# DMA transposes in place of TensorE transposes for attention outputs and expert products, in a two-layer macaron block

## The chip, the cores and the metric

The kernel is one program on one core of a Trainium2 chip. The metric is the time of an execution on the device in microseconds (us); several executions are timed, and the median is compared.

## The reference

The input is `x`, 4 sequences of 512 tokens, 128 wide, in 32 bits. Every stage adds to `x` (LN is a layer norm without weights):

```python
x = x + 0.5 * ffn(LN(x))       # W1, W2 made ternary; 128 -> 512 -> 128, relu
x = x + attn0(LN(x))           # RMS norm, 16 heads of 64, causal, gated by sigmoid(x @ Wg)
x = x + 0.5 * ffn(LN(x))       # the same weights again
x = x + 0.5 * moe(LN(x))       # 8 experts, the top 2 of each token
x = x + attn1(LN(x))           # layer norm with gamma and beta, 16 heads of 64, causal
x = x + 0.5 * moe(LN(x))       # the same experts
```

In attention, `out = softmax(q k^T) v` of all heads is laid side by side (1024 wide) and multiplied by `Wout` (1024 to 128). In `moe`, an expert computes `h = silu(xs @ W1[e]) * (xs @ W3[e])`, 512 wide, and `y = h @ W2[e]`, where `xs` is the token times its softmax weight; `y` is added to the token.

## The kernel before

**Numbers.** Matrix products are nearly as precise as 32 bits, in 16-bit operands: every operand is split into a high 16-bit part (a cast, mostly on ScalarE) and a low one (the value less the high part, on VectorE or GpSimd), and a product is three matmuls: high by high, high by low, low by high (`split_mm`, L1696 to L1703). The matmul contracts over the partitions, so the stationary operand must have the contracted axis on its partitions: a result that lies token by token has to be transposed before it can be multiplied by the next weight. TensorE does this with a matmul against the identity in 32 bits, from SBUF into PSUM; then ScalarE casts the transposed high part out of PSUM, and VectorE subtracts for the low one.

**Order of the work.** Each engine runs its own stream of instructions, written out by hand in the same shape, and semaphores tie them together. The stages are: first feed-forward; `attention(0)`; `moe(0)`; `attention(1)`; `moe(1)`. Norms, the second feed-forward, the routing and the loading of weights are put into turns of the attentions (tables `FILL`, `STATS`) and into iterations of the expert loops (`carried`). DMAs are issued by SyncE (SP) in one stream, the gathers and scatters of the expert tiles by GpSimd (POOL).

**Attention.** An item is one pair of heads of one sequence: 4 x 8 = 32 items. There are 36 turns t. In turn t item t is projected to q, k and v (`p`), item t-1 has its row maxima (`m`), item t-2 its scores and exponentials (`s`), item t-3 its outputs (`v`), item t-4 its output projection (`o`). TensorE's order in a turn is:

```python
scores(0); maxima(0); project_q(); project_k()  # k here, unless late_k
turn_outputs()                                  # L1926: 4 transposes of O32 into PSUM bank 7
scores(1); maxima(1)                            # scores(1) waits for the first exponential (L972)
project_k()                                     # here if late_k: a turn with no entry in FILL
project_v(); filled(); scores(2); maxima(2)
outputs(0); max_rows(); outputs(1); project_out()
```

`turn_outputs` (L1929) waits for VectorE to have divided the outputs of the turn before into `O32` (L1361). ScalarE casts the high part (`turned_high`, L1005), after its first exponential (L972) and the casts of q. VectorE makes the low part (`turned_low`, L1332) in its order after the second group of maxima (`maxima(1)`, L1308) and before the third. `project_out` (L1933) waits for that low part, `s_otl_sb`, and multiplies by `WOh` and `WOl` (L1698 to L1700). The PSUM banks 6 and 7 hold the outputs; bank 7 holds the transposed outputs in between, so `outputs(1)` waits for `s_otl_sb` of the item before (L1913). GpSimd makes most casts and low parts of the exponentials (L782, L784).

**Experts.** Tokens are sorted by expert into tiles of 128 rows, 46 tiles for each `moe`. GpSimd gathers the rows of a tile (L835) four tiles ahead and scatters the results eight iterations later (`OUT_LAG`, L843). In iteration t of `run_tiles` (L535) the stages run with lags 0, 1, 2 and 3: `turned_token` (TensorE transposes the tile, ScalarE and VectorE split it), `up` (two `split_mm` of 512 columns into banks 1 and 2; ScalarE's `gate`, L1124, applies silu, VectorE's `product`, L1662, multiplies into `G32`), `turned_product` (L2128: four 32-bit transposes into bank 3 or 4; ScalarE's `product_high`, L1130; VectorE's `product_low`, L1668) and `down` (twelve matmuls, L2140 to L2142; ScalarE's `result`, L1138). `up` of a tile waits for the gate and the product of the tile before, since all tiles use the same two banks.

**SyncE.** Its stream loads inputs and weights (L564 to L592), stores normalised tokens as rows in HBM for the gathers (L610), loads the expert results (L618) and stores the output (L603, L630), each behind a wait for its data.

## Time and profile before

| | us |
|---|---|
| three runs | 1001.63, 1004.79, 1005.98 |
| median | 1004.79 |
| span of the profiled execution (first to last instruction) | 1000.9 |
| attention(0), turns 0 to 35, roughly | 35 to 363 |
| moe(0) | 364 to 526 |
| attention(1) | 526 to 839 |
| moe(1) | 840 to 989 |
| busy: TensorE, VectorE, GpSimd, ScalarE | 897, 792, 735, 674 |

The profiled execution's own time is its span and what lies around it, which isn't shown apart; the span is 3.9 us below the median of the runs. An engine's busy time counts its instructions from start to end; TensorE's matmuls overlap, so a row of four may be "busy" for less than four times one. "PEld" is the load of the stationary operand. A row of the timeline has start, duration, engine, line, operation, what is written and read, and the count of merged instructions; in brackets stands how long the engine was idle before, and which instruction ended that.

### The profile page before, as it was taken

What the parts mean: (1) busy time and instruction counts of PE and PEld (TensorE: products, weight loads), DVE (VectorE), ACT (ScalarE), POOL (GpSimd) and SP (SyncE); (2) the same over time, 40 slices, a digit from 0 to 9 for tenths busy, and PEclk for the clock granted to TensorE, in tenths of its full rate; (3) what the DMA queues carried; (4) which work ended last, traced back from release to release, by engine and by line L of the source; (5) the groups of instructions that cost most, each with busy time, mean ns of one, the idle gap of its engine ahead of it and who ended that gap; (6) DMA issues with size and microseconds to landing.
All of it is one profiled execution on the core that took longest, in us unless ns stands there. A gap on an engine that the chain in (4) does not pass through costs nothing.

```text
span 1000.9 us, 33897 instructions
## 1 busy us (share of the span) xinstructions
PE 897.1 (90%) x13160; PEld 640.5 (64%) x13160; DVE 792.1 (79%) x2394; ACT 673.5 (67%) x1183; POOL 734.7 (73%) x685
## 2 busy tenths in 40 slices
PE   5789999999999879899987899999999985998884
PEld 3467676776777656566654676777677764666663
DVE  6889898888889877777656889888888887866563
ACT  6688888878877626556555787767767762545552
POOL 6789989889887745666545999878888883666662
PEclk9999999999999979999999999999999997999997
DMA  5201011010030001122111000000000001121222
GB/s 153 78 10 45 3 45 45 3 45 2 3 107 3 2 20 39 52 43 85 38 30 51 3 3 3 12 3 2 13 3 3 13 2 30 41 43 44 86 62 82
DMA packets 21118, 33.79 MB, mean 34 GB/s; under 512 B 4578, under 2 KB 10466, under 8 KB 20964
## 3 DMA queue, kind: packets, MB, share of 16 engines
q1 hardware_dynamic: 13728, 18.50, 5.9%
q0 software_dynamic: 5888, 12.07, 4.8%
q8 instruction: 110, 1.80, 0.8%
q10 hardware_dynamic: 1348, 1.05, 0.3%
q14 instruction: 44, 0.36, 0.1%
HBM read 22.44 MB, written 9.18 MB: 32 GB/s over the span
## 4 chain that ended last, share of the span: by engine, by line
PE 63%; DVE 18%; ACT 6%; issue 6%; POOL 3%; another core or an unknown queue 2%; DMA 1%; SPq 0%; POOLq 0%; DVEq 0%; ACTq 0%
PE ps L1698 8%; PE ps L1889 8%; PE ps L1700 8%; PE ps L1699 7%; DVE arena L1308 4%; PE ps L1919 3%; PE ps L2128 3%; PE ps L1853 3%; PE ps L1920 3%; PE ps L1921 3%; PE ps L2140 2%; PE ps L2141 2%; PE ps L2142 2%; PE ps L1864 2%
## 5 line engine op out<-in xcount | busy, mean ns | idle before, releaser
L784 POOL TENSOR_TENSOR arena<-arena 128x1024 f16<-128x1024 f32 x190 | 344.9, 1816 | 86.2 <-ACT arena L980 75.9
L1308 DVE CUSTOM_DVE_ANT_0 arena<-ps,mask_qk 128x512 bf16<-128x512 f32 (+3 forms) x512 | 224.4, 485 | 25.0 <-PE ps L1853 23.8
L972 ACT ACTIVATE arena<-ps,lift 128x1024 f32<-128x1024 f32 (+1 forms) x192 | 186.7, 972 | 85.0 <-PE ps L1899 82.2
L1889 PE MATMUL ps<-arena 64*128 64x512 f16 (+3 forms) x1536 | 148.5, 299 | 10.2 <-ACT arena L972 6.8
L835 POOL DMA_INDIRECT arena<-x_rows,arena x92 | 92.6, 1006 | 88.5 <-PE ps L2103 43.7
L1919 PE MATMUL ps<-arena 128*128 128x65 f16 x1280 | 130.9, 195 | 0.2 <-DVE arena L1332 0.2
L1920 PE MATMUL ps<-arena 128*128 128x64 f16 x1280 | 130.4, 193 | 0.0
L1921 PE MATMUL ps<-arena 128*128 128x65 f16 x1280 | 130.0, 194 | 0.0
L843 POOL DMA_INDIRECT y_rows<-arena x92 | 90.8, 987 | 49.0 <-ACT arena L1138 26.1
L1919 PEld LDWEIGHTS ps<-arena 128*128 128x128 f16 x1280 | 117.4, 98 | 8.4 <-issue 0.5
L1920 PEld LDWEIGHTS ps<-arena 128*128 128x128 f16 x1280 | 117.9, 99 | 0.2 <-issue 0.2
L1921 PEld LDWEIGHTS ps<-arena 128*128 128x128 f16 x1280 | 117.9, 98 | 0.0
L782 POOL CAST arena<-arena 128x1024 f16<-128x1024 f32 x124 | 103.6, 835 | 0.0
L1662 DVE SCALAR_TENSOR_TENSOR arena<-ps,arena 128x512 f32<-128x512 f32 x92 | 68.8, 748 | 29.1 <-ACT arena L1124 16.0
L1889 PEld LDWEIGHTS ps<-arena 64*128 64x128 f16 x1536 | 52.1, 94 | 53.1 <-ACT arena L972 22.3
L1668 DVE TENSOR_TENSOR arena<-ps,arena 128x512 f16<-128x512 f32 x92 | 63.1, 686 | 26.1 <-ACT arena L1130 18.4
L1130 ACT ACTIVATE arena<-ps 128x512 f16<-128x512 f32 x92 | 55.3, 601 | 42.1 <-PE ps L2128 24.7
L2140 PE MATMUL ps<-E2h,arena 128*128 x368 | 71.4, 222 | 11.1 <-DVE arena L1668 6.0
L1124 ACT ACTIVATE arena<-ps,arena 128x512 f32<-128x512 f32 x92 | 63.4, 689 | 18.5 <-PE ps L1700 15.1
L1853 PE MATMUL ps<-arena 64*128 64x512 f16 (+3 forms) x512 | 66.2, 296 | 7.7 <-DVE arena L1308 6.6
L2142 PE MATMUL ps<-E2h,arena 128*128 x368 | 71.1, 219 | 0.0
L2141 PE MATMUL ps<-E2l,arena 128*128 x368 | 71.0, 219 | 0.0
(288 smaller groups left out, 2695.9 us busy)
## 6 DMA issues: line engine op xcount, KB each, us to landing
stage<-in_L_ffn_W SPq DMA_DIRECT2D x4, 1024.0 KB, 5.3
arena<-y_rows SPq DMA_DIRECT2D x14, 256.0 KB, 3.6
x_rows<-XN SPq DMA_DIRECT2D x8, 256.0 KB, 2.1
arena<-x_rows,arena POOLq DMA_INDIRECT x92
y_rows<-arena POOLq DMA_INDIRECT x92
stage<-in_L_attn_Wkv SPq DMA_DIRECT2D x2, 512.0 KB, 8.3
X<-in_L_attn_tokens SPq DMA_DIRECT2D x3, 256.0 KB, 5.1
out_x<-X SPq DMA_DIRECT2D x3, 256.0 KB
```

What stands on the lines that cost most here:

```text
L782: g.tensor_copy(PH[:, b, :, cols], P32[:, :, cols]).then_inc(s_ph_pool, 1)
L784: g.tensor_tensor(PL[:, b, :, cols], P32[:, :, cols], PH[:, b, :, cols], ALU.subtract).then_inc(s_pl, 1)
L835: g.indirect_dma_start(XG[:, t % XRING, :], None, x_rows[t // HT], bass.IndirectOffsetOnAxis(ap=row_i[:, 0, t:t + 1], axis=0)).then_inc(s_ ...
L972: a_.activation(P32[:, :, UNIT_AT[u]:UNIT_AT[u] + UNIT_W[u]], ps[:, 4:6, 0:UNIT_W[u]], ACT.Exp, bias=lift[:]).then_inc(s_ex_p, 1)
L1308: v_.tensor_tensor_reduce(masked[:, x, 0:w], ps[:, 2 + x, at:at + w], mask_qk[:, CH - w:CH], 1.0, NEG, ALU.add, ALU.max, accum_out=MX[:, i ...
L1853: ins_ = mm(ps[:, 2 + x, at:at + (i + 1) * P], QKh[rows, r, 0, i * P:(i + 1) * P], QKh[rows, r, 1, 0:(i + 1) * P], start=(n_ == 0), stop=( ...
L1889: mm(ps[:, 4 + x, at:at + w], keys, queries, start=(n_ == 0 and part == 0), stop=False)
L1919: mm(ps[:, 6 + x, c:c + DH + 1], ph_, VH[:, r, k, x, 0:DH + 1], start=(k == 0), stop=False)
L1920: mm(ps[:, 6 + x, c:c + DH], ph_, VL[:, r, k, x, :], start=False, stop=False)
L1921: ins_ = mm(ps[:, 6 + x, c:c + DH + 1], pl_, VH[:, r, k, x, 0:DH + 1], start=False, stop=(k == i))
L2140: mm(dst, GH[:, g, f, :], wh, start=(f == 0), stop=False)
L2142: ins_ = mm(dst, GL[:, g, f, :], wh, start=False, stop=(f == HB - 1))
```

## The change

1. **Attention outputs.** `turn_outputs` is gone. ScalarE and VectorE split `O32` as it lies, in SBUF, into `OS` (high and low side by side, 128 x 1024 in 16 bits). SyncE then issues one DMA transpose from `OS` to `OT`, which lies in the space of `T32`, and `project_out` waits for its landing. The lags between the stages of an item stay as they are, and so do the places of the two splits in ScalarE's and VectorE's order. `outputs(1)` no longer waits.
2. **Expert products.** `turned_product` is gone. ScalarE and VectorE split `G32` into `GS` (a ring of 3), in iteration t+2, SyncE issues one DMA transpose of 128 x 1024 to `GT` (a ring of 4), and `down` and `result` move from lag 3 to lag 4; the scatter's lag goes from 8 to 9. The banks freed (3 and 4) make `up` alternate between two pairs, so that it waits for the gate and product of two tiles before.
3. **SyncE's stream** is written in turns and tiles: the loads and stores that used to follow each other stand between the transposes.
4. The affine step of the norm before the second attention works in place in PSUM, since `T32` is taken.

```diff
-        GRING = 3
+        GRING = 4
+        SRING = 3
...
-        OTh = carve([CH], F16)
-        OTl = carve([CH], F16)
+        OS = carve([2, CH], F16)
+        OT = T32[:].bitcast(F16).rearrange("p (k i d) -> p k i d", k=2, i=TPB)
...
-        TLAGS = (0, 1, 2, 3)
-        OUT_LAG = 8
+        DOWN_LAG = 4
+        OUT_LAG = 9
...
+        def up_banks(t):
+            return 1 + 2 * (t % 2), 2 + 2 * (t % 2)
```

SyncE, new:

```diff
+            def attention(a):
+                base = a * ITEMS
+                def body(t):
+                    o = items(t)[4]
+                    if o is not None:
+                        j = base + o
+                        sp.wait_ge(s_o_lo, j + 1)
+                        if j >= 1:
+                            sp.wait_ge(s_op_ps, j)
+                        sp.dma_start_transpose(OT.rearrange("p k i d -> p (k i) d"), OS.rearrange("p k c -> p (k c)")
+                                               ).then_inc(s_o_turned, 16)
+                    if a == 0 and t == 0:
+                        expert_block(0)
+                    if a == 0 and t == 1:
+                        expert_block(1)
+                    if a == 0 and t in (6, 10, 14, 18):
+                        expert_block((t - 6) // 4 + 2)
+                    if a == 0 and t == 27:
+                        second_layer()
+                    if t in ROWS_OUT[a]:
+                        rows_out(*ROWS_OUT[a][t])
+                run_items(body, range(TURNS))
+            ROWS_OUT = ({20: (3, 0), 28: (3, 1)}, {13: (5, 0), 21: (5, 1), 29: (5, 2)})
...
+            def moe(m):
+                for t in range(ETILES):
+                    w = ETILES * m + t
+                    sp.wait_ge(s_g_lo, w + 1)
+                    if t >= GRING:
+                        sp.wait_ge(s_y_ps, w - GRING + 1)
+                    sp.dma_start_transpose(GT[:, t % GRING].rearrange("p k f d -> p (k f) d"),
+                                           GS[:, t % SRING].rearrange("p k h -> p (k h)")
+                                           ).then_inc(s_g_turned[t % GRING], 16)
+                    if m == 0 and t == 4:
+                        rows_out(3, 2)
+                    if m == 0 and t == 7:
+                        rows_out(3, 3)
+                    if m == 1 and t == 0:
+                        rows_out(5, 3)
+                    if t == 31:
+                        results_in(m, 0)
+                    if m == 1 and t == 38:
+                        stored(0)
+                    if m == 1 and t == 41:
+                        stored(1)
+            attention(0)
+            moe(0)
+            results_in(0, 1)
+            attention(1)
+            moe(1)
```

ScalarE and VectorE:

```diff
-                        act.wait_ge(s_ot_ps, j + 1)
-                        if o >= 1:
-                            act.wait_ge(s_op_ps, j)
-                        a_.activation(OTh, ps[:, 7, :], ACT.Copy).then_inc(s_oth_sb, 1)
+                        act.wait_ge(s_o_ev, j + 1)
+                        if j >= 1:
+                            act.wait_ge(s_o_turned, 16 * j)
+                        a_.activation(OS[:, 0], O32.rearrange("p a x d -> p (a x d)"), ACT.Copy).then_inc(s_o_hi, 1)
...
-                    act.wait_ge(s_gt_ps, w + 1)
-                    if t >= GRING:
-                        act.wait_ge(s_y_ps, w - GRING + 1)
-                    a_.activation(GH[:, t % GRING].rearrange("p a b -> p (a b)"), ps[:, 3 + t % 2, :], ACT.Copy
-                                  ).then_inc(s_g_hi, 1)
+                    act.wait_ge(s_g32_rdy, w + 1)
+                    if t >= SRING:
+                        act.wait_ge(s_g_turned[(t - SRING) % GRING], moved(m, (t - SRING) % GRING, t - SRING + 1))
+                    a_.activation(GS[:, t % SRING, 0], G32[:, t % 2, :], ACT.Copy).then_inc(s_g_hi, 1)
...
-                run_tiles(m, (token_high, gate, product_high, result), carried)
+                run_tiles(m, ((token_high, 0), (product_high, 2), (gate, 1), (result, DOWN_LAG)), carried)
...
-                        dve.wait_ge(s_oth_sb, base + o + 1)
-                        v_.tensor_tensor(OTl, ps[:, 7, :], OTh, ALU.subtract).then_inc(s_otl_sb, 1)
+                        dve.wait_ge(s_o_hi, base + o + 1)
+                        v_.tensor_tensor(OS[:, 1], O32.rearrange("p a x d -> p (a x d)"), OS[:, 0], ALU.subtract
+                                         ).then_inc(s_o_lo, 1)
...
-                run_tiles(m, (token_low, product, product_low, None), carried)
+                run_tiles(m, ((token_low, 0), (product_low, 2), (product, 1)), carried)
```

TensorE:

```diff
-                    def turn_outputs():
...
-                        pe.wait_ge(s_otl_sb, base + o + 1)
+                        pe.wait_ge(s_o_turned, 16 * (base + o + 1))
...
-                    if o is not None:
-                        turn_outputs()
...
-                    if t >= 1:
-                        pe.wait_ge(s_a_sb, w)
+                    a_bank, b_bank = up_banks(t)
+                    if t >= 2:
+                        pe.wait_ge(s_a_sb, w - 1)
...
-                def turned_product(t, w):
...
-                    pe.wait_ge(s_g_lo, w + 1)
+                    pe.wait_ge(s_g_turned[g], moved(m, g, t + 1))
...
-                run_tiles(m, (turned_token, up, turned_product, down), carried)
+                run_tiles(m, ((turned_token, 0), (up, 1), (down, DOWN_LAG)), carried)
```

## Rows read from the trace of the kernel before

**Rows 1.** The page, chain that ended last: shares of the span by engine.

```profile
PE 63%; DVE 18%; ACT 6%; issue 6%; POOL 3%; another core or an unknown queue 2%; DMA 1%; SPq 0%; POOLq 0%; DVEq 0%; ACTq 0%
```

**Rows 2.** Stretches: length, busy us (instructions) of five engines, granted clock, DMA share, GB/s.

```profile
100.00:340.00 240.00, 233.72 (x4172) 168.68 (x4168) 211.00 (x702) 197.62 (x309) 210.06 (x173) 1.00 0.09 27
...
375.00:520.00 145.00, 131.03 (x1139) 92.53 (x1138) 102.08 (x255) 83.89 (x200) 86.00 (x93) 0.98 0.18 50
545.00:800.00 255.00, 246.54 (x4520) 180.91 (x4521) 224.81 (x730) 190.66 (x283) 215.66 (x173) 1.00 0.02 6
848.00:985.00 137.00, 125.90 (x1081) 87.80 (x1080) 92.14 (x207) 74.32 (x181) 82.84 (x84) 1.00 0.21 55
```

**Rows 3.** Timeline, attention(1), turn 16, which has no filler block.

```profile
667.45 1.11 ACT L972 ACTIVATE arena<-ps,lift 128x1024 f32<-128x1024 f32 x1 [1.49 <-PE ps L1899]
...
668.23 0.60 PE L1929 MATMUL ps<-ident,arena 128*128 128x128 f32 x4
...
668.76 0.28 PEld L1889 LDWEIGHTS ps<-arena 64*128 64x128 f16 x6 [0.17 <-ACT arena L972]
...
671.51 0.69 DVE L1332 TENSOR_TENSOR arena<-ps,arena 128x512 f16<-128x512 f32 x1
...
674.22 0.22 PE L1698 MATMUL ps<-WOh,arena 128*128 128x128 f16 x1
```

**Rows 4.** Timeline, attention(1), turn 14, which has a filler block.

```profile
648.82 1.11 ACT L972 ACTIVATE arena<-ps,lift 128x1024 f32<-128x1024 f32 x1 [1.49 <-PE ps L1899]
...
650.24 0.60 PE L1929 MATMUL ps<-ident,arena 128*128 128x128 f32 x4
...
650.77 0.34 PE L1889 MATMUL ps<-arena 64*128 64x384 f16 x2
```

**Rows 5.** Timeline, attention(0), turn 10, whose scores wait for the exponential.

```profile
122.85 1.10 ACT L972 ACTIVATE arena<-ps,lift 128x1024 f32<-128x1024 f32 x1
...
124.01 0.28 PEld L1889 LDWEIGHTS ps<-arena 64*128 64x128 f16 x6 [0.35 <-ACT arena L972]
```

**Rows 6.** Groups by line: shapes, count | busy us, mean ns of one | idle before.

```profile
L1332 DVE TENSOR_TENSOR arena<-ps,arena 128x512 f16<-128x512 f32 x64 | 43.9, 686 | 4.4 <-ACT arena L1005 4.4
...
L1005 ACT ACTIVATE arena<-ps 128x512 f16<-128x512 f32 x64 | 38.0, 594 | 7.7 <-PE ps L1929 7.7
...
L918 ACT ACTIVATE stage<-stage 128x512 f32<-128x512 f32 x24 | 15.1, 627 | 0.0
...
L1286 DVE TENSOR_TENSOR X<-X,arena 128x512 f32<-128x512 f32 x6 | 4.1, 686 | 0.1
```

**Rows 7.** The page, DMA issues: queue, count, KB each, median us from issue to landing.

```profile
stage<-in_L_ffn_W SPq DMA_DIRECT2D x4, 1024.0 KB, 5.3
arena<-y_rows SPq DMA_DIRECT2D x14, 256.0 KB, 3.6
x_rows<-XN SPq DMA_DIRECT2D x8, 256.0 KB, 2.1
...
stage<-in_L_attn_Wkv SPq DMA_DIRECT2D x2, 512.0 KB, 8.3
```

**Rows 8.** Timeline, attention(0), the last turn.

```profile
361.38 0.68 DVE L1332 TENSOR_TENSOR arena<-ps,arena 128x512 f16<-128x512 f32 x1
...
362.12 0.29 PE L1698 MATMUL ps<-WOh,arena 128*128 128x128 f16 x1
```

**Rows 9.** Groups by line: the transposes of the expert products.

```profile
L2128 PE MATMUL ps<-ident,arena 128*128 128x128 f32 x368 | 55.7, 274 | 7.5 <-issue 4.8 <-DVE arena L1668 2.7
```

**Rows 10.** Timeline of GpSimd, moe(1): a scatter, then a gather.

```profile
921.57 0.99 POOL L843 DMA_INDIRECT y_rows<-arena  x1 [0.30 <-issue]
922.86 0.97 POOL L835 DMA_INDIRECT arena<-x_rows,arena  x1 [0.30 <-issue]
```

**Rows 11.** Waits in 375 to 520 us, then in 848 to 985 us: total us, times, longest.

```profile
POOL arena L835 <- PE ps L2103: 22.0, 23, 2.2
...
POOL arena L835 <- PE ps L2103: 21.3, 22, 2.1
```

More of the change, by code:

```diff
@@ L342, in macaron_block @@
         s_o_ev = sem("o_ev")
[L343 to L345 removed]
+        s_o_hi = sem("o_hi")
+        s_o_lo = sem("o_lo")
+        s_o_turned = sem("o_turned")
         s_op_ps = sem("op_ps")
@@ L530, in macaron_block @@
         KEY_AT = {k: UNIT_AT[u] + at for u, unit in enumerate(EXP_UNITS) for k, at in unit}
-        TLAGS = (0, 1, 2, 3)
-        OUT_LAG = 8
+        DOWN_LAG = 4
+        OUT_LAG = 9
         def run_tiles(m, stages, carried):
-            for t in range(ETILES + TLAGS[-1]):
-                for f, lag in zip(stages, TLAGS):
-                    if f is not None and 0 <= t - lag < ETILES:
+            for t in range(ETILES + DOWN_LAG):
+                for f, lag in stages:
+                    if 0 <= t - lag < ETILES:
                         f(t - lag, ETILES * m + t - lag)
                 carried(m, t)
+        def up_banks(t):
+            return 1 + 2 * (t % 2), 2 + 2 * (t % 2)
         def second_weights(i):
@@ L574, in _, with expert_block @@
             sp.dma_start(wg_in[:, HEADS:HEADS + EXPERTS], ins["L1_ffn_Wg"]).then_inc(s_wa_in[4], 16)
-            for i, (src, hi, lo) in enumerate(experts):
+            def expert_block(i):
+                src = experts[i][0]
                 if i == 0:
@@ new lines, in rows_out, with results_in @@
+            def rows_out(n, c):
+                sp.wait_ge(s_ln_xn, NORM_NO[n, c])
+                at = c % HCH * CH
+                sp.dma_start(x_rows[c // HCH][at:at + CH].rearrange("(p t) d -> p t d", t=TPC),
+                             XN[:, TPC * c:TPC * (c + 1), :]).then_inc(s_x_rows[c // HCH], 16)
+            def results_in(m, h):
+                for k in range(YRING):
+                    sp.wait_ge(s_y_out[k], moved(m, k, HT * (h + 1)))
+                for c in range(HCH * h, HCH * (h + 1)):
+                    for j in range(TOPK):
+                        at = j * TOK + c * CH
+                        sp.dma_start(Yt[:, c, j], y_rows[at:at + CH].rearrange("(p t) d -> p t d", t=TPC)
+                                     ).then_inc(s_y_got[c], 16)
@@ L1187, in turned_x @@
                 elif n == 4:
-                    step(v_.tensor_scalar(T32[:], src, gamma[:], beta[:], ALU.mult, ALU.add))
-                    ins_ = v_.tensor_tensor(l, T32[:], h, ALU.subtract)
+                    step(v_.tensor_scalar(src, src, gamma[:], beta[:], ALU.mult, ALU.add))
+                    ins_ = v_.tensor_tensor(l, src, h, ALU.subtract)
                 else:
@@ L1924, in outputs @@
                             ins_.then_inc(s_av_ps, 1)
-                    def turn_outputs():
-                        pe.wait_ge(s_o_ev, base + o + 1)
-                        for i in range(TPB):
-                            ins_ = nc.tensor.transpose(ps[:, 7, i * P:(i + 1) * P],
-                                                       O32[:, i].rearrange("p x d -> p (x d)"), ident[:])
-                        ins_.then_inc(s_ot_ps, 1)
                     def project_out():
-                        pe.wait_ge(s_otl_sb, base + o + 1)
+                        pe.wait_ge(s_o_turned, 16 * (base + o + 1))
                         if o == 0 and a == 0:
```

94 lines of the change are left out of this document (31 added, 63 removed).

## The prediction, made before the changed kernel ran

> **What bounds the kernel now.** I read the chain of work that ended last first, then busy times by stage, then single turns and tiles in the timeline. The chain lies mostly on TensorE [rows 1]. By stage [rows 2] the two attentions (100 to 340 us and 545 to 800 us) have TensorE busy for 234 of 240 us and 247 of 255 us, with VectorE at 211 and 225 and GpSimd at 210 and 216; the two expert stages have it busy for 131 of 145 and 126 of 137 us. So the TensorE work that the change takes out is nearly all on the path, and the question is what is late once it is gone. Two things matter for that: what TensorE waits for right behind the removed transposes, and how long after the low part of the outputs is ready TensorE wants the transposed copy.
>
> **Removed in attention.** Each turn loses four 32-bit transposes (L1929). They hold TensorE for 0.53 us, from their start to that of the scores behind them: 668.23 to 668.76 [rows 3] and 650.24 to 650.77 [rows 4]. What that is worth depends on the exponential (L972) that those scores wait for. In a turn without a filler block, it ends at 667.45 + 1.11 = 668.56 and the scores begin 0.20 us later [rows 3]; where they plainly wait for it, they begin 0.06 us after it (122.85 + 1.10 = 123.95, scores at 124.01) [rows 5]. So only 0.14 us of the 0.53 can be had. In a filled turn it ended at 649.93, 0.84 us before the scores [rows 4], and all 0.53 are had. Read turn by turn, of the 56 turns that have scores and outputs together (turns 4 to 31 of either attention) 31 are like rows 4, 18 like rows 3 and 7 like rows 5: 31 x 0.53 + 18 x 0.14 + 0 = **-19 us**.
>
> **Kept on the other engines.** ScalarE's and VectorE's halves now read O32 in SBUF in place of a PSUM bank. ScalarE takes 594 ns for 128x512 from PSUM and 627 ns in SBUF; VectorE 686 ns either way [rows 6]. Nothing on the path; if their cover went, it would be 64 x 0.03 = 2 us. The rewritten affine step of the second attention's norm works in PSUM in place of T32, four times over: nothing. Dropping the wait before the second half of the outputs frees nothing, since that wait was met several us before.
>
> **Added in attention.** SyncE issues one 128x1024 16-bit transpose (256 KB) per turn once the low part is done, and the projection (L1698 with WOh) waits for it to land. The low part still comes after the second maxima on VectorE, and the projection still ends the turn: the low part ends at 671.51 + 0.69 = 672.20, the projection starts at 674.22 [rows 3]. That window of 2.02 us is all the cover the transfer has, and it doesn't move when the transposes go, since both ends hang on TensorE work behind them. Of the 56 turns 51 have 1.87 to 2.02 us and five have 2.66 to 4.01 us. With L the time from the low part to the projection's release, every turn grows by L - 2.0 if L is longer. TensorE works in order: behind the waiting projection stand the next turn's scores, and so its exponentials and maxima. None of it is hidden.
>
> **L.** No row shows a transposing transfer or one within SBUF. Of the same size and queue, the store of the normalised tokens to HBM lands 2.1 us after issue and the load of expert results into SBUF 3.6 us; far off, 512 KB of weights take 8.3 us, and 1 MB takes 5.3 us [rows 7]. A transfer of 256 KB that is also reordered should not beat 2.1. I take **3.6** (same size, same queue, ends in SBUF) plus 0.1 for SyncE to see the semaphore and issue, so L = 3.7, with ends at 2.1 and 8.3. At 3.7 the 51 turns cost about 1.73 each and the other five 3.2 in all: **+92 us**. Turns 32 to 35 have windows of 2.1 to 6.0 us, except the last of each attention, whose projection follows the low part at once (361.38 + 0.68, projection at 362.12) [rows 8]: 2 x 3.6 there and 6.6 in the other six, **+14 us**. The Trainium skill (DMA: Bandwidth & Descriptors, the anatomy of one DMA, which it gives for the gpsimd path) prices a DMA at about 2.0 us plus bytes over 436 GB/s, 2.6 us for 256 KB; by it the whole sum would come out at about +5 us instead of +68. The rows lie on both sides of that.
>
> **Experts.** Each of the 92 tiles loses four transposes (one lasts 274 ns [rows 9], four in a row 0.60 us as four of the same form do in attention [rows 3], so each adds 0.11 and four 0.44 us of streaming), 40 us in all, and gets two more PSUM banks, so that a tile's first products need not wait for the gate of the tile before. But GpSimd issues a gather and a scatter for each tile, 0.99 + 0.30 + 0.97 + 0.30 = 2.56 us [rows 10], while the shortest TensorE tile is 2.52 us. Where tiles are that short already, nothing is gained. Gain comes from the longer ones (282 us for some 87 tiles, 3.2 on average), at most the 22.0 + 21.3 us that GpSimd's gathers wait for TensorE [rows 11]. Ends 0 and 43; as part of the stretch is landing of scatters and carried work, I take a little over half, **-24 us**. The transfer itself is covered: the product's low part is made two iterations before the down projection, some 4.8 us, and L is 3.7. At the end of either stage nothing covers it: L in place of 0.6 of transposes and some slack, 2 x 2.5 = **+5 us**.
>
> SyncE's queue: weight blocks, token rows, result loads and stores now stand between transposes, each placed at a turn at which what it waits for is done. They issue in 0.3 to 0.9 us, about nine us apart from the next transpose in attention. Costed at nothing; if a 1 MB block shares the DMA engines with a transpose, the five turns that issue weights grow by at most 5.3 us each, 27 us, in the upper end.
>
> **Sum.** -19 + 92 + 14 - 24 + 5 = +68 us. The profiled execution has a span of 1000.9 us, 3.9 below the median of the runs (1004.79); 1000.9 + 68 + 3.9 = **1073 us**. TensorE's clock: the expert stages, with TensorE idle for 14 of 145 and 11 of 137 us in gaps of up to some two us, were granted 0.98 and 1.00, which is the 2.4 GHz level nearly throughout [rows 2]. Gaps of 1.7 us a turn are charged nothing; at longer L they could add.
>
> **Rivals.**
> 1. *The transfer lands in its window (faster).* If L is 2.1, as the store's row has it, the 56 turns cost 7 and give back 19, the last turns cost 4, the experts give 24 and lose 1: -31, **974 us**. For it: the row exists, and the transfer touches no HBM. Against: it is the fastest row of its size, and a transpose scatters what it writes. It decides at L of about 2.6, where the attention's loss (+20) equals the experts' gain.
> 2. *The crossbar is slow.* Blocks of 128x128 go through one after the other, and L is 8.3, as the slowest row. Attention then costs 349 + 48 - 19 = +378, the down projection waits until two tile periods cover 8.6 us (4.3 against 3.2, 87 tiles, +95), the ends 2 x 7 = 14: **about 1490 us**. Nothing in the trace speaks for or against. The Trainium skill (VectorE: DVE Perf Modes, the three transpose paths) has the crossbar at 1309 ns for one 128x128 16-bit block against 390 ns on TensorE and advises TensorE where PSUM will do; eight blocks in a row would be 10.5 us, worse still, while if most of 1309 ns is paid once, it is rival 1 or the forecast. No run here shows it yet.
> 3. *TensorE's transposes were hidden anyway.* True for 25 of 56 turns, and in the sum. If it holds in the experts too (GpSimd the bound), their 24 us go, and the time is 1097: inside the forecast.
>
> **How the numbers follow.** Forecast (L from 2.6 to 5.3, from 1005 to about 1180): 0.59. Rival 1: 0.22. Rival 2 or anything with L above 5.3: 0.19. For the range I cut a tenth at either end: at L = 2.4 and a full expert gain about 985; at L = 6 the turns cost 225, the ends about 40 and the experts gain nothing, about 1235. A change of 0.5% (5 us) is about what can be told from none here. Faster by more: all of rival 1 but its edge, 0.20; within: 0.05; slower: 0.75.
>
> **What would show it.** In the changed profile the projection's first matmul should wait for the transposing DMA in nearly each turn, for about 1.7 us, and turns grow from 8.6 to 9.3 us to about 10.2; the DMA list should have its landing near 3.6 us; the scores should follow the exponential by 0.06 us in unfilled turns. Expert tiles should sit near 2.6 to 3.0 us with the down projection rarely waiting for the DMA. The forecast is wrong if landing is under 2.6 or over 5.3 us, if the window of two us has moved, or if the expert stages grow.

## The result, and the profile of the changed kernel

| | before | after |
|---|---|---|
| runs | 1001.63 to 1007.53 (4) | 1088.19 to 1096.77 (4) |
| median, us | 1005.38 | 1090.29 |
| span of the profiled execution | 1000.9 | 1089.1 |

The ratio is 1.0858, with a 95% interval from 1.0816 to 1.0901: slower by 85 us, where the forecast was slower by 68 (1073 us). Start with the page of the changed kernel: busy time of the engines, DMA packets, the largest queue, the chain that ended last by engine and by line.

```profile
PE 869.2 (80%) x12536; PEld 582.4 (53%) x12536; DVE 801.4 (74%) x2394; ACT 672.5 (62%) x1183; POOL 743.4 (68%) x685
...
q1 hardware_dynamic: 178464, 59.42, 27.0%
...
PE 37%; DVE 23%; DMA 22%; ACT 7%; issue 6%; another core or an unknown queue 4%; POOL 1%; SPq 0%; ACTq 0%; POOLq 0%; DVEq 0%
DMA T<-arena 18%; DVE arena L1368 8%; PE ps L1949 8%; PE ps L1758 6%; PE ps L1760 5%; PE ps L1759 4%; DVE arena L1392 4%; DMA arena<-arena 3%; ACT arena L1032 2%; PE ps L1913 2%; PE ps L1954 1%; PE ps L2180 1%; DVE bst L1234 1%; PE ps L2181 1%
```

TensorE is busy for 869 us instead of 897 and yet the chain lies on it for 37% of the span where it was 63% [rows 1]; DMA went from 1% to 22%, nearly all of it the transpose of the attention outputs (`T<-arena`; the experts' is `arena<-arena`). The waits (us in total, times, longest) say where it bites:

```profile
PEld ps L1758 <- DMA T<-arena: 92.2, 61, 4.5
PE ps L1758 <- DMA T<-arena: 85.0, 61, 4.4
ACT arena L1198 <- remote: 51.1, 22, 5.5
```

L1758 with `WOh` is the projection's first matmul. It waits for the transpose in 61 of 64 turns, for 85 us in all. By stretches, like [rows 2] (length, busy us of five engines, granted clock, DMA share, GB/s): attention(0), moe(0), attention(1), moe(1).

```profile
100.00:370.00 270.00, 231.41 (x4128) 160.98 (x4122) 218.31 (x707) 198.90 (x311) 213.69 (x175) 0.98 0.24 49
410.00:560.00 150.00, 121.37 (x957) 75.63 (x955) 101.65 (x257) 83.22 (x201) 90.22 (x94) 0.94 0.59 123
600.00:900.00 300.00, 253.29 (x4575) 176.61 (x4575) 239.71 (x775) 195.95 (x290) 224.57 (x178) 0.98 0.16 30
935.00:1070.00 135.00, 108.77 (x856) 66.40 (x855) 88.13 (x202) 71.26 (x174) 82.19 (x81) 0.99 0.69 139
```

TensorE is now idle for 39 of 270 and 47 of 300 us in the attentions (before 6 of 240 and 8 of 255), and the DMA share of the expert stages is 0.59 and 0.69 where it was 0.18 and 0.21. The stages, each up to the end of its last projection or down projection on TensorE: attention(0) 37.5 us longer, moe(0) 5.2, attention(1) 42.9, moe(1) 2.7, together the 88.2 us by which the span grew. So the attentions lost 80 us (forecast: 92 + 14 - 19 = 87), and the experts lost 8 where they should have gained 19.

**One turn.** Turn 15 of attention(1), in the timeline: low part, issue, first matmul of the projection.

```profile
714.54 0.69 DVE L1392 TENSOR_TENSOR arena<-arena 128x512 f16<-128x512 f32 x1
...
715.26 1.23 SPq L631 DMA_TRANSPOSE T<-arena  x1
...
718.06 0.23 PE L1758 MATMUL ps<-WOh,T 128*128 128x128 f16 x1 [0.65 <-DMA T<-arena]
```

The low part ends at 714.54 + 0.69 = 715.23, the projection starts at 718.06: L, the time from the one to the other, is 2.83 us, against a window of 2.02 [rows 3]. The data move late in this time. The DMA traffic in 717 to 718 us:

```profile
DMA  9999999999999999542100000000000000000000
GB/s 297 287 317 256 307 276 317 276 276 297 297 297 266 277 216 185 103 83 41 21 10 0 0 0 0 0 0 0 0 0 0 0 0 0 0 0 0 0 0 0
DMA packets 491, 0.12 MB, mean 118 GB/s; under 512 B 491, under 2 KB 491, under 8 KB 491
```

By the records of the packets there are 1024 of 256 bytes, from 716.43 to 717.53, and 32 of 4 bytes, the last at 717.53; TensorE starts 0.53 us later. That is 1.2 us from issue to the first packet, 1.1 moving, 0.5 to the consumer. Now turn 16, which should be the same:

```profile
723.86 0.69 DVE L1392 TENSOR_TENSOR arena<-arena 128x512 f16<-128x512 f32 x1
...
724.57 1.23 SPq L631 DMA_TRANSPOSE T<-arena  x1
...
729.09 0.29 PE L1758 MATMUL ps<-WOh,T 128*128 128x128 f16 x1 [2.36 <-DMA T<-arena]
729.28 0.31 PE L1760 MATMUL ps<-WOh,T 128*128 128x128 f16 x1
```

L = 4.54. The DMA traffic of 726.6 to 727 us, then that of 728 to 728.03 us, shows why:

```profile
DMA packets 166, 0.05 MB, mean 128 GB/s; under 512 B 165, under 2 KB 165, under 8 KB 165
...
q1 hardware_dynamic: 165, 0.03, 42.2%
q8 instruction: 1, 0.02, 20.0%
```

```profile
DMA packets 2, 0.00 MB, mean 0 GB/s; under 512 B 2, under 2 KB 2, under 8 KB 2
...
q1 hardware_dynamic: 2, 0.00, 9.4%
```

All data had landed at 726.83, as early after the issue as in turn 15. But a block of 16 KB of instructions for an engine (q8) began at 726.74 and lasted until 728.02, and two of the 32 four-byte packets came only then, at 728.00 and 728.01. The projection started 1.08 us after those two, where it had started 0.53 us after the last small packet in turn 15; what the further half microsecond is, the records don't show. The Trainium skill (DMA: Bandwidth & Descriptors, why a DMA increments its semaphore by 16) says that each DMA engine that takes part, here up to 16, writes its own completion after its data, and that only the full count of 16 means that all has landed. The records agree as far as they go: there are 32 small packets, twice 16, and one late pair holds the projection. They don't say which DMA engine a packet was on. The projection's matmuls also took 0.31 us here against 0.22 to 0.23 in turn 15. The stretches at the two projections (columns as above) show the granted clock, full speed or 2.4 GHz in turn 15, half of it or 1.2 GHz in turn 16, after TensorE had stood for 2.36 us and not 0.65; the forecast had this at nothing.

```profile
718.00:719.00 1.00, 0.94 (x14) 0.79 (x16) 1.00 (x3) 0.00 (x0) 0.92 (x2) 1.00 0.00 0
729.00:730.00 1.00, 0.91 (x9) 0.91 (x10) 0.00 (x0) 0.00 (x0) 1.00 (x1) 0.50 0.00 0
```

**All 56 turns** with scores and outputs together, by when a 16 KB block of instructions began:

| turns | instruction block begins, us after the issue | L, us | above 2.83, summed |
|---|---|---|---|
| 26 | none between the issue and the landing (in four turns one had begun 0.3 to 1.3 before the issue) | 2.81 to 2.92 | 0.3 |
| 13 | 0.15 to 0.73: data late; in 12 of them the issue itself is longer, 1.56 to 2.58 us | 3.16 to 4.25 | 10.2 |
| 7 | 1.0 to 1.8: data late, to 3.2 to 4.4 us | 3.85 to 5.07 | 9.9 |
| 8 | 2.1 to 2.4: data in time, the last completion late | 4.30 to 4.63 | 12.9 |
| 2 | none, or after the landing | 3.02, 3.16 | 0.5 |

Mean L is 3.43, the sum 192.3 us. Against each turn's own window before (115.7 in all) that is **76.6 us** more. In turns 5 to 31 of either attention L took 74.6 us more than the windows, and the turns grew by 57.4. A block holds up more than one DMA engine in sixteen would explain: in 14 turns 513 to 541 of the 1024 data packets, and all 32 small ones, came after the time at which they land undisturbed.

**The clock in the attentions.** Between the first and the last projection of both attentions TensorE was granted the lower of its two levels, 1.2 GHz, for 49 us in the changed kernel and for 7 us before (added up from the granted clock in the two traces). At half speed at most half of the difference is lost time: an estimate of up to 21 us of the 80, part of which may lie in stretches in which TensorE waited anyway. No run here parts this from the waits.

### The profile page after: what moved, and what is told of

Read it like the earlier page. It is cut to its first block, busy times and chain, and to the rows that moved or that the text cites. A ratio compares the mean times of both kernels' runs of the same rounds, so it can differ in the third digit from the quotient of the medians.

```text
span 1089.1 us, 32863 instructions
## 1 busy us (share of the span) xinstructions
PE 869.2 (80%) x12536; PEld 582.4 (53%) x12536; DVE 801.4 (74%) x2394; ACT 672.5 (62%) x1183; POOL 743.4 (68%) x685
## 4 chain that ended last, share of the span: by engine, by line
PE 37%; DVE 23%; DMA 22%; ACT 7%; issue 6%; another core or an unknown queue 4%; POOL 1%; SPq 0%; ACTq 0%; POOLq 0%; DVEq 0%
DMA T<-arena 18%; DVE arena L1368 8%; PE ps L1949 8%; PE ps L1758 6%; PE ps L1760 5%; PE ps L1759 4%; DVE arena L1392 4%; DMA arena<-arena 3%; ACT arena L1032 2%; PE ps L1913 2%; PE ps L1954 1%; PE ps L2180 1%; DVE bst L1234 1%; PE ps L2181 1%
## 5 line engine op out<-in xcount | busy, mean ns | idle before, releaser
L1949 PE MATMUL ps<-arena 64*128 64x512 f16 (+3 forms) x1536 | 153.9, 307 | 15.9 <-ACT arena L1032 13.1
L903 POOL DMA_INDIRECT y_rows<-arena x92 | 95.3, 1036 | 50.0 <-ACT arena L1198 27.2
L1758 PE MATMUL ps<-WOh,T 128*128 128x128 f16 x256 | 49.6, 229 | 88.1 <-DMA T<-arena 85.0
L2180 PE MATMUL ps<-E2h,arena 128*128 x368 | 77.6, 229 | 42.8 <-ACT arena L1198 21.7
L1198 ACT ACTIVATE arena<-ps 128x128 f32<-128x128 f32 x92 | 25.5, 277 | 97.8 <-remote 51.1
L1434 DVE SCALAR_TENSOR_TENSOR X<-ps,X 128x512 f32<-128x512 f32 x64 | 44.1, 688 | 48.3 <-PE ps L1760 48.1
L2182 PE MATMUL ps<-E2h,arena 128*128 x368 | 76.9, 226 | 0.0
L1758 PEld LDWEIGHTS ps<-WOh,T 128*128 128x128 f16 x256 | 25.8, 101 | 95.4 <-DMA T<-arena 92.2
L1728 DVE TENSOR_TENSOR arena<-arena 128x512 f16<-128x512 f32 x92 | 63.5, 690 | 18.0 <-ACT arena L1191 11.1
```

The source lines that it names most:

```text
L903: g.indirect_dma_start(y_rows, bass.IndirectOffsetOnAxis(ap=row_i[:, 1, t:t + 1], axis=0), YS[:, t % YRING, :], None).then_inc(s_y_out[t % ...
L1758: mm(dst, sh, mh, start=True, stop=False)
L1949: mm(ps[:, 4 + x, at:at + w], keys, queries, start=(n_ == 0 and part == 0), stop=False)
L2180: mm(dst, GT[:, g, 0, f, :], wh, start=(f == 0), stop=False)
```

## The experiments

Every time is compared with the kernel before, run in the same round. That one took 969.14 us in the round of the `e_` runs, 1008.19 in that of the `f_` runs and 968.54 in that of the `g_` runs and of `f_mid_split` (the last two rounds have the same chip number on record), so the ratios count, not the microseconds. The difference lies in the expert stages (below, 8 and 11); turns of attention agree between the rounds within 0.1 us on average. Where an experiment "leaves out the turning", the projection (or the down projection) multiplies by data that lie token by token.

**1 and 2: one half of the change each.** In `e_att_dma` the experts are as before, in `e_moe_dma` the attention is.

```diff
 # e_att_dma: experts as before
-            return 1 + 2 * (t % 2), 2 + 2 * (t % 2)
+            return 1, 2
-                run_tiles(m, ((turned_token, 0), (up, 1), (down, DOWN_LAG)), carried)
+                run_tiles(m, ((turned_token, 0), (up, 1), (turned_product, 2), (down, DOWN_LAG)), carried)
 # e_moe_dma: attention as before
+                    if o is not None:
+                        turn_outputs()
                     if s is not None:
                         scores(1)
```

> Attention by DMA transpose as in the change, experts back on TensorE's transposes with the old lags and banks. Theory A (the wait of the output projection for the transfer is the loss): the two attentions grew by 37 and 43 us in the changed kernel's trace, so before + 80 = 1085 us, with the projection's first matmul waiting for the DMA in nearly every turn. Theory B (the loss comes from the transfers sharing the DMA engines in the expert stages and from the longer lag there): the attentions alone would cost 20 us or less, 1025 us.

> The other half alone: experts by DMA transpose with banks in pairs and lag 4, attention back on TensorE's transposes. Theory A: the expert stages grew by 6 and 4 us in the trace, so before + 10 = 1015 us. Theory B: most of the 85 us, so 1070 us. The recorded forecast had a gain of 19 us for this half, 986 us.

Attention alone: 1051.14 us, ratio 1.0858 (1.0812 to 1.0904), the whole loss. Its turns take 10.76 and 10.26 us, the median L is 3.37. Experts alone: 972.89 us, ratio 1.0027 (0.9995 to 1.0060): no gain, where the forecast had 19 us. The stretch 830 to 960 us of `e_moe_dma`, and its waits there:

```profile
830.00:960.00 130.00, 112.49 (x915) 70.33 (x913) 90.60 (x207) 72.88 (x181) 87.95 (x86) 0.95 0.80 152
```

```profile
ACT arena L1190 <- PE ps L2185: 47.2, 45, 4.9
...
POOL y_rows L895 <- ACT arena L1190: 12.8, 14, 1.9
POOL arena L887 <- PE ps L2154: 11.2, 11, 2.0
PE ps L2183 <- DMA arena<-arena: 10.7, 9, 3.5
```

The down projection (L2183) does wait for the transpose at times, 10.7 us in this stretch, TensorE is granted 0.95 and the DMA engines are busy for 0.80 of the time.

**3 and 4: the split early.** The high part goes to the head of ScalarE's turn and the low part behind the first maxima, so that the window grows from 2.0 us to 4.8 on average (4.3 at least). `e_early_moe_pe` is the same with the experts on TensorE.

```diff
+                    if o is not None:
+                        output_high()
                     if s is not None:
                         exps(0)
...
                     if m is not None:
                         maxima(0)
+                    if o is not None:
+                        output_low()
                     if p is not None:
                         q_low()
```

> The changed kernel with the split of the outputs moved ahead: the high part at the head of ScalarE's turn, before the first exponential, the low part on VectorE after the first pair of maxima. The window before the projection grows from 2.0 to about 4.4 us, the transfer stays what it is (2.8 us, up to 5 when a load of instructions meets it). Theory A: nearly all waits of the projection for the DMA go, and the removed transposes give their 19 us: 1005 - 19 + 2 (waits left) + 8 (last turns) + 10 (experts) = 1006 us. Theory B (the transfer costs time wherever it runs, since it delays the loads of instructions and of weights): the turns stay above 10 us, 1060 us or more. Theory C (VectorE cannot do the low part so early without delaying the maxima): projection no longer waits, but turns grow by 0.3 to 0.7 us, 1020 to 1045 us.

> Early split in attention, experts back on TensorE. Theory A: 1005 - 19 + 2 + 8 = 996 us, faster than both kernels. Theory B: 1050 us. Theory C: 1010 to 1035 us. The difference from the run with early split and expert DMAs says again what the experts' half costs, 10 us by theory A.

998.45 us, ratio 1.0296 (1.0271 to 1.0320), and 993.38 us, 1.0242 (1.0216 to 1.0267). That is theory C of both expectations, and neither theory A. With the transfer covered, 5.6 and 6.2 of the 8.6 points come back (per cent of the time), so most of the loss was the uncovered transfer and what came with it. Of the rest, the waits show one part that the shift itself makes (`e_early_moe_pe`, waits; then its low part by line):

```profile
ACT arena L1059 <- DVE arena L1417: 31.6, 30, 3.9
...
PE ps L1754 <- DVE arena L1370: 20.3, 38, 1.1
```

```profile
L1387 DVE TENSOR_TENSOR arena<-arena 128x512 f16<-128x512 f32 x64 | 59.4, 928 | 1.7 <-ACT arena L1059 1.6
```

ScalarE now waits at its head for `O32` (L1417), the low part of q (L1370) comes later, so that TensorE waits 20.3 us for it where it waited 3.6 in `e_att_dma`, and the low part of the outputs takes 928 ns on average, not the 686 of [rows 6]. TensorE also had 23 us at the lower clock in these attentions (52 in `e_att_dma`), so the clock may be in the rest too.

**5 and 9: no turning at all.** Attention without transposes and without the DMA; the projection reads `OS` as it lies. In `g_free_ps` the low part reads a PSUM bank (other data) in place of `O32`, and the second half of the outputs waits for it again, as before the change. The experts are as before in both.

```diff
-                        sp.dma_start_transpose(OT.rearrange("p k i d -> p (k i) d"), OS.rearrange("p k c -> p (k c)")
-                                               ).then_inc(s_o_turned, 16)
...
-                        pe.wait_ge(s_o_turned, 16 * (base + o + 1))
+                        pe.wait_ge(s_o_lo, base + o + 1)
 # g_free_ps, besides
-                        v_.tensor_tensor(OS[:, 1], O32.rearrange("p a x d -> p (a x d)"), OS[:, 0], ALU.subtract
+                        v_.tensor_tensor(OS[:, 1], ps[:, 7, :], OS[:, 0], ALU.subtract
```

> Attention without any transpose of the outputs (the projection reads them untransposed, so its values are others; experts as before the change): removes both the TensorE transposes and the DMA. The recorded forecast priced the removed transposes at 19 us of some 1005, so a ratio of 0.981 to the kernel before. Rival (another engine's order bounds the turn): ratio 0.995 or more.

> The attention without transposes and DMA again, but VectorE's low part reads PSUM bank 7 in place of O32 in SBUF (other values; the second half of the outputs waits for it, as before the change). In the run that read SBUF, 12 of 64 low parts took 0.9 to 2.3 us in place of 0.69, mean 832 ns, where they ran beside GpSimd's subtraction. Theory F (two SBUF operands collide with GpSimd, and that ate part of the 19 us): mean back at 0.69 us, 9 us gained, ratio 0.986 to 0.988 in place of 0.995. Rival (the collisions lie in VectorE's slack): 0.995 again.

1005.97 us, ratio 0.9954 (0.9932 to 0.9975), and 957.85 us, 0.9893 (0.9875 to 0.9911): the first is its rival, the second near theory F. So the removed transposes alone are worth 10 us (0.0107 x 968.54), not 19, and with the split in SBUF 5 (0.0046 x 1008.19; 2 by the difference of the medians, and in another round, so rough). The traces say the same by themselves: against the trace before, the 54 turns 5 to 31 are shorter by 13.5 us in `g_free_ps` and by 6.5 in `f_att_free`. In `g_free_ps` 18 of them are shorter by 0.43 or 0.44 us, six by 0.29 to 0.35, ten by 0.13 or 0.14 and 16 by nothing; three are shorter by 0.8 to 1.3 and one is longer by 0.6. The low part of `f_att_free`, then that of `g_free_ps`:

```profile
L1383 DVE TENSOR_TENSOR arena<-arena 128x512 f16<-128x512 f32 x64 | 53.3, 832 | 4.6 <-ACT arena L1055 4.6
```

```profile
L1383 DVE TENSOR_TENSOR arena<-ps,arena 128x512 f16<-128x512 f32 x64 | 43.9, 686 | 4.6 <-ACT arena L1055 4.6
```

Turn 14 of attention(0) in `f_att_free` shows one such case, VectorE and GpSimd:

```profile
165.07 1.76 DVE L1383 TENSOR_TENSOR arena<-arena 128x512 f16<-128x512 f32 x1
```

```profile
163.88 1.16 POOL L733 TENSOR_TENSOR E3l<-stage,E3h 128x512 f16<-128x512 f32 x1
165.01 1.27 POOL L723 TENSOR_TENSOR X<-X,b2h 128x512 f32<-128x512 f32 x1
```

The low part began 0.06 us after GpSimd's instruction, and ended 0.55 us after that one's end: as if it had stood still for that time. It is so each time: all 11 low parts of `f_att_free` over 0.72 us, the nine of the changed kernel and the 36 of `f_mid` began during a GpSimd instruction and ended 0.54 to 0.55 us after its end, and in `g_free_ps` none is over 0.70 us. The Trainium skill has this (SBUF — State Buffer, two separate sides, and who interferes with whom): a VectorE instruction with two inputs in SBUF is blocked for the whole of a GpSimd instruction that reads SBUF and started first, one with at most one input there is not. Both runs agree with it, 832 ns against 686.

**6, 7 and 12: the transfer split, and the split moved a little.** `f_split` turns the high half as soon as it is there and the low half after it; `f_mid` makes the low part before the second maxima instead of after them; `f_mid_split` does both. The experts are on TensorE.

```diff
 # f_split
+                        sp.wait_ge(s_o_hi, j + 1)
+                        sp.dma_start_transpose(OT[:, 0], OS[:, 0]).then_inc(s_o_turned, 16)
+                        sp.wait_ge(s_o_lo, j + 1)
+                        sp.dma_start_transpose(OT[:, 1], OS[:, 1]).then_inc(s_o_turned, 16)
 # f_mid
+                    if o is not None:
+                        output_low()
                     if m is not None:
                         maxima(1)
```

> Attention by DMA, experts on TensorE, but two transposes of 128x512 per turn: the high part as soon as it is cast, the low part when it is ready. Theory A1 (the 2.8 us are 1.0 to the first packet, 1.1 of moving 256 KB and 0.7 to the release; only the middle scales with size): the wait of each turn falls by 0.55 us, 56 to 64 turns, 33 us, ratio 1.053 in place of 1.086. Theory A2 (it is a fixed cost per transfer, and the queue is shared): no gain, 1.08 to 1.10, as the second transfer waits behind the first.

> Attention by DMA, experts on TensorE, the low part made on VectorE before the second group of maxima instead of behind it, the high part left where the change has it. The window grows from 2.0 to 3.4 us. Theory A (window): clean turns lose their whole 0.8 us of wait and the slow ones 1.4, 60 us in all: ratio 1.025. Theory C (VectorE's order): the second maxima come 0.35 to 0.7 us late and TensorE waits for them in the third group, so a third of it is given back: 1.04 to 1.05.

> Attention by DMA, experts on TensorE, low part before the second maxima and two half transposes: the two edits that each helped. If the wait is the loss, the clean turns are covered already by the earlier low part (window 3.4 to 3.7 us against 2.8) and only those that meet a load of instructions gain: ratio 1.020 to 1.027 in place of 1.030. If the two add up in full: 1.003. If the second transfer only loads the queue: 1.035.

1067.10 us, 1.0586 (1.0543 to 1.0630); 1040.60 us, 1.0303 (1.0250 to 1.0355); 997.63 us, 1.0300 (1.0279 to 1.0320). The first is near its theory A1, the second between its two theories, and the third, where `f_mid` was, is none of its three. Half the data frees the projection 0.4 us earlier (2.41 us after the low part undisturbed): it moves in 0.8 us and not 1.1, and the rest stays. In `f_mid` the window is 3.7 us and the waits for the transpose are nearly gone (4 of 64, 4.9 us), yet 3 points remain, and the split transfer adds nothing to it: something else bounds those. `f_mid`, turn 16 of attention(1), then what TensorE waits for in the whole run:

```profile
693.13 1.48 DVE L1387 TENSOR_TENSOR arena<-arena 128x512 f16<-128x512 f32 x1
```

```profile
PEld ps L1909 <- DVE arena L1363: 48.1, 70, 1.4
PE ps L1909 <- DVE arena L1363: 40.8, 68, 1.3
```

The low part, again beside a GpSimd subtraction (L838, 692.90 to 694.06), pushes VectorE's second maxima (L1363) out, and TensorE's maxima (L1909), in the same banks, wait for them in 68 places, 40.8 us in all, where `e_att_dma` has 3.5. In its old place the low part delayed nobody in this way.

**10: a plain copy.** The same 256 KB, same queue, same place, not turned.

```diff
-                        sp.dma_start_transpose(OT.rearrange("p k i d -> p (k i) d"), OS.rearrange("p k c -> p (k c)")
+                        sp.dma_start(OT.rearrange("p k i d -> p (k i d)"), OS.rearrange("p k c -> p (k c)")
```

> Attention by DMA, experts on TensorE, the transposing transfer replaced by a plain copy of the same 128x1024 from OS to OT (so the projection reads untransposed outputs; other values). Theory G (it is the fixed cost of any transfer): release after 2.1 to 2.8 us, ratio 1.06 to 1.086. Theory H (the crossbar makes it long): release within 2.0 us, ratio 1.00 to 1.01.

1001.68 us, ratio 1.0327 (1.0293 to 1.0361). Its issues on SyncE, then those of the transposes in the changed kernel (ns, min/median/max):

```profile
L630 SPq DMA_DIRECT2D T<-arena x64: 464/465/523, 70.8 to 850.7; - x64
...
DMA to landing us min/median/max: 2.3/2.3/4.6
```

```profile
L631 SPq DMA_TRANSPOSE T<-arena x64: 1232/1233/2582, 70.8 to 918.4; - x64
```

A plain transfer frees the projection in 2.35 us undisturbed, 2.78 on average; the transposing one in 2.81 and 3.43 (3.47 in `e_att_dma`). The release is as theory G has it, but the ratio lies between the two theories: 5.3 of the 8.6 points belong to the transposing form. It takes 0.8 us more for its issue, partly made up by a shorter rest, and an instruction block holds up more of it: in ten turns of `g_copy` exactly 8 of the 128 data packets and 1 of the 16 small ones are late, a sixteenth, as if one DMA engine were held, while in the transposing form half of the packets and all small ones are (above). TensorE's time at the lower clock in the attentions is 21 us here, 52 in `e_att_dma`.

**8 and 11: the experts.** `f_moe_free` leaves out the turning there (no transpose, no DMA; attention as before). `g_spscat` also stores the results as whole blocks from SyncE, in place of GpSimd's scatter.

```diff
-                        sp.dma_start_transpose(GT[:, t % GRING].rearrange("p k f d -> p (k f) d"), ...
...
-                    pe.wait_ge(s_g_turned[g], moved(m, g, t + 1))
+                    pe.wait_ge(s_g_lo, w + 1)
 # g_spscat, besides
-                        g.indirect_dma_start(y_rows, bass.IndirectOffsetOnAxis(ap=row_i[:, 1, t:t + 1], axis=0),
-                                             YS[:, t % YRING, :], None).then_inc(s_y_out[t % YRING], 16)
+                    sp.wait_ge(s_y_sb, w + 1)
+                    sp.dma_start(y_rows[blk * P:(blk + 1) * P], YS[:, t % YRING, :]).then_inc(s_y_out[t % YRING], 16)
```

> Attention as before the change; experts with banks in pairs and lag 4, but with neither the TensorE transposes nor the DMA (the down projection reads the untransposed product, so its values are others). Theory D (the transposes' gain is real and the transfers' sharing of the DMA engines, which were 60 to 80% busy, eats it): 20 to 30 us faster, ratio 0.97 to 0.98, against 1.003 with the transfers. Rival E (GpSimd's issue of a gather and a scatter, 2.56 us a tile, bounds the tile, so that there was nothing to gain): ratio 0.99 to 1.00.

> Experts without transposes as in the earlier run (ratio 0.996), and the results stored by SyncE as plain contiguous blocks in place of GpSimd's indirect scatter (other rows, so other values), which takes 1.3 us a tile off GpSimd. Rival E (GpSimd's two descriptor writes a tile bound the experts): tiles fall from 3.1 to 2.0 to 2.4 us, 92 tiles, 60 us or more, ratio below 0.95. Theory D (TensorE's own waits bound them): ratio 0.98 to 0.996.

1004.04 us, ratio 0.9960 (0.9941 to 0.9979): with all 92 x 4 transposes gone and nothing in their place, 4 us are gained, as rival E has it. 942.43 us, ratio 0.9735 (0.9716 to 0.9754): without the scatter, 26 us. GpSimd in moe(1) of `f_moe_free`:

```profile
899.32 0.97 POOL L882 DMA_INDIRECT arena<-x_rows,arena  x1 [0.30 <-issue]
900.59 0.99 POOL L890 DMA_INDIRECT y_rows<-arena  x1 [0.30 <-issue]
902.93 0.97 POOL L882 DMA_INDIRECT arena<-x_rows,arena  x1 [1.36 <-remote]
904.21 1.00 POOL L890 DMA_INDIRECT y_rows<-arena  x1 [0.30 <-issue]
905.51 0.97 POOL L882 DMA_INDIRECT arena<-x_rows,arena  x1 [0.30 <-issue]
```

Two tiles take 905.51 - 899.32 = 6.19 us, 3.1 each: four indirect DMAs with their issue are 5.1, and before every second gather stands a wait of 1.36 us and not of 0.30. That wait belongs to the rounds in which the kernel before takes 1005 to 1008 us. In those at 969 no gather waits for "remote"; `e_att_dma`, whose experts are those before the change, in moe(1):

```profile
927.58 0.97 POOL L889 DMA_INDIRECT arena<-x_rows,arena  x1 [0.30 <-issue]
928.85 0.99 POOL L897 DMA_INDIRECT y_rows<-arena  x1 [0.31 <-issue]
930.15 0.97 POOL L889 DMA_INDIRECT arena<-x_rows,arena  x1 [0.30 <-issue]
```

That is 2.57 us a tile, which is also the median from gather to gather there (3.09 in the trace of the kernel before). So GpSimd's sequence is full in either kind of round. It is also where the rounds differ: from first to last gather the two unchanged expert stages take 146.1 + 139.6 us in `f_att_free` and 129.8 + 116.8 in `g_free_ps`, 39 us less, as much as lies between 1008 and 969. With the scatter off GpSimd, the gather again waits for TensorE, 56.3 us in 120 (`g_spscat`, 800 to 920 us), and a tile takes 2.58 us on average and 2.47 in the median over both expert stages, with many at 2.08 in moe(1):

```profile
POOL arena L885 <- PE ps L2149: 56.3, 40, 3.1
```

It was expected below 0.95 by rival E; it ended at 0.9735, since TensorE comes next, at 2.1 to 2.6 us a tile.

No version with a DMA transpose beat the kernel before. Those that did leave work out.

## Why the prediction was right, and where it was not

**The +92 for the turns** was right in kind: the projection waits for the transfer in nearly each turn, the window of two us did not move, and nothing hides the rest. Measured: 76.6 us, at a mean L of 3.43 against 3.7. But L is no single value. The fixed part, 2.83 us, would cost 43 us in 56 turns; the other 34 stand in the turns in which an instruction block meets the transfer. The rows of the sum, the 2.1 us of a store and the 3.6 of a load [rows 7], were medians of few transfers and said nothing of instruction blocks: that 3.7 came near the mean of 3.43 was in part luck.

**The +14 for the last turns:** the eight waits grew by 13.6 us over their windows, the turns by 16.5. The other 6 us of the 80 lie before turn 5, some 2 of them in the projection of turn 4.

**The -19** was too large. In the trace of the changed kernel 74.6 us more of L against 57.4 of growth leave 17.2 saved, but that is a remainder: it also holds what the clock and longer low parts cost. Measured alone it is 10 us in `g_free_ps` (13.5 in the turns of its trace) and 5 in `f_att_free`. Two steps were off. The 0.53 us of a filled turn came out as 0.43 or 0.44, and "7 like rows 5" were 16 in which nothing came, among them turns 7 to 10, 12, 13 and 19 to 21 of attention(0); the 0.14 of an unfilled turn came out in ten turns. And "VectorE 686 ns either way" [rows 6] did not hold: the row with both inputs in SBUF, L1286, is of six instructions at a place where no GpSimd instruction held them up. Beside GpSimd's work the mean was 803 ns in the changed kernel, up to 2.13 us.

**The -24 and +5 for the experts** was the wrong step: measured +8 in the trace of the changed kernel and 1.0027 for that half alone, 22 us off. "A little over half" of what GpSimd's gathers wait for TensorE [rows 11] took those waits for slack. Even with the transposes simply gone they give 4 us. GpSimd's gather and scatter fill the tile: at 2.57 us, the 2.56 of [rows 10], in the rounds at 969, and at 3.1 us in those at 1005 to 1008, as the prediction's trace is, where every second gather waits a further us that those two rows do not show. That was rival 3, which had no chance of its own; by it the sum was 1097, with 1090.29 measured. By the prediction's own signs the forecast was wrong here: the expert stages grew.

**The sum and its errors.** +68 was forecast and +85 measured. The attentions were 7 us under their forecast and the experts 22 to 27 over theirs, so the two errors partly cancel in the total. The ends of the range don't follow from the prediction's own terms either: at L = 2.4 with the full expert gain they add up to about 973 and not 985, at L = 6 to about 1250 and not 1235. The measured time is inside either way.

**Rival 1** (L 2.1) fell: not even a plain copy gets under 2.3. **Rival 2** (L 8.3) fell too: eight blocks moved in 1.1 us. The 1309 ns for one block of the Trainium skill (VectorE: DVE Perf Modes, the three transpose paths) was thus not a price to multiply, as the rival's own last sentence allowed. The Trainium skill's formula for a DMA of the gpsimd path (DMA: Bandwidth & Descriptors, the anatomy of one DMA), an estimate of 2.6 us for 256 KB, lies between the 2.3 of the copy and the 2.8 of the transpose, both from SyncE.

**Priced at nothing and not nothing:** the clock, 0.98 in the attentions where it was 1.00, and 0.94 in moe(0) where it was 0.98. In the attentions it fell after waits like that of turn 16, and up to 21 us may hang on it (estimated above). **At nothing and so far right:** SyncE's order. The five turns in which a row store follows the transpose have L of 3.28 to 4.63, but an instruction block met each of them too, and no run here parts the two.

**Left open.** What the extra us before every second gather waits for (the profile says "remote"), and why it is there in some rounds and not in others. How much of the loss in turns is the instruction blocks' doing by experiment: they were matched turn by turn with late packets, not varied. How much of it is the clock.

## What to carry to other kernels

Moving work from a busy engine to a DMA pays only where the time from the producer to the consumer covers the DMA's latency with its disturbances: here 2.8 us undisturbed and 3.4 on average, and nearly all waits were gone at a window of 3.7. Read that window first, in a turn of the timeline, and cost what is missing as a full loss, since an engine that runs in order stands still. Where the window can be widened only by moving the producer, look at what its new place delays. And before work is taken off an engine that seems the bound, add up the issue times of the quiet engine beside it over several periods, not one.

## What the runs showed of the hardware

- One transposing DMA of 128x1024 in 16 bits inside SBUF: 1.23 us on SyncE's queue, data in 1.1 us (240 GB/s, up to some 300 at a time), the consumer starts 2.8 us after the producer ends. 128x512 (`f_split`) takes 1.19 us for its issue, so that hardly depends on the size; a plain copy of 256 KB takes 0.47 us for it (`g_copy`).
- Blocks of 16 KB of instructions took 0.9 to 1.4 us each, at most 2.0, and transfers that met one were late. One that met the moving data of the transposing DMA delayed half of its packets and all its small ones; in the plain copy it was a sixteenth of either. One that came 2.1 to 2.4 us after the issue found all data landed and still held the consumer for 1.5 to 1.8 us, with one late pair of small packets of 32.
- A 128x512 subtraction with both inputs in SBUF took 686 ns alone. Where it began during a GpSimd instruction it ended 0.55 us after that one, after up to 2.3 us (`f_att_free`). With one input in PSUM it took 686 ns throughout (`g_free_ps`).
- When gathers and scatters of GpSimd went back to back, every second gather waited 1.3 to 1.4 us and the one between 0.30 (`f_moe_free`, and the traces of both kernels have such waits); in the rounds at 969 us all waited 0.30 (`e_att_dma`).
